# One instruction block for the whole program, and a new instruction order and PSUM plan in the third stage

## The reference, cut to what matters

```python
x = x + self_attention(_layernorm(x))                 # 16 heads of 8
x = x + cross_attention(_layernorm(x), ctx, mask)     # 16 heads of 64
x = x + ffn(_layernorm(x))                            # ffn below

def ffn(x):
    for i in range(6):
        x = attn_layer(shift_tokens(x), Wqkv[i], q_scale[i], k_scale[i], Wo[i]) + x
        x = ffn_layer(shift_tokens(x), ln_g[i], ln_b[i], W1[i], b1[i], W2[i], b2[i]) + x
    return x

def attn_layer(x, Wqkv, qs, ksc, Wo):      # 16 heads of 64, causal window of 32
    q, k, v = split(x @ Wqkv)
    q, k = l2norm(q) * qs, l2norm(k) * ksc
    q = q * cos * scale + rotate_half(q) * sin * scale
    k = k * cos / scale + rotate_half(k) * sin / scale
    return local_attention(q, k, v) @ Wo   # softmax(8 q k + mask) v

def ffn_layer(x, g, bln, W1, b1, W2, b2):
    a, gate = split(layernorm(x) * g + bln) @ W1 + b1
    return a * gelu(gate) @ W2 + b2
```

## Time and profile before

| what | value |
|---|---|
| median of 3 runs | 3522.41 us |
| profiled execution, device time | 3525.89 us |
| its span, first to last instruction | 3524.1 us |
| PE busy / weight loads | 96% / 71% |
| DVE, ACT, POOL busy | 80%, 79%, 70% |
| mean granted TensorE clock | 0.993 |

### The profile page before, as it was taken

The page is one execution under the profiler, slowest core; times in us unless marked ns, Lnnn a source line. Parts: engine busy times, 40 slices in busy tenths (PEclk is TensorE's granted clock), DMA queues, the critical chain, the costliest instruction groups (busy, mean ns, idle before and its releaser), DMA issues.

```text
span 3524.1 us, 120975 instructions
## 1 busy us (share of the span) xinstructions
PE 3377.9 (96%) x49605; PEld 2495.3 (71%) x49605; DVE 2811.5 (80%) x5297; ACT 2792.7 (79%) x5522; POOL 2475.5 (70%) x4812
## 2 busy tenths in 40 slices
PE   8989997999999999999999999999999999999997
PEld 5778774677777777777777777777777777777776
DVE  6834445888888888888888888888888888888885
ACT  5756664688888888888888888888888888888885
POOL 5622224777777777777777777777777777777774
PEclk9999998999999999999999999999999999999999
DMA  3000002444444444444444444444444444444441
GB/s 101 3 10 8 9 6 50 92 82 82 82 81 89 95 82 82 80 88 97 82 82 82 83 90 93 82 82 80 90 96 83 82 82 88 78 85 83 88 85 39
DMA packets 200382, 260.17 MB, mean 74 GB/s; under 512 B 123161, under 2 KB 145438, under 8 KB 199838
## 3 DMA queue, kind: packets, MB, share of 16 engines
q0 software_dynamic: 55296, 201.35, 30.4%
q1 hardware_dynamic: 143820, 50.88, 5.8%
q10 hardware_dynamic: 722, 0.21, 0.0%
HBM read 23.95 MB, written 2.10 MB: 7 GB/s over the span
## 4 chain that ended last, share of the span: by engine, by line
PE 78%; issue 2%; DVE 1%; POOL 1%; DMA 1%; ACT 0%; SPq 0%; POOLq 0%; DVEq 0%
PE bank L1032 18%; PE bank L1008 16%; PE bank L1083 10%; PE bank L1160 10%; PE bank L1128 7%; PE bank L1144 6%; PE bank L1103 5%; PE bank L1024 3%; PE bank L1098 2%; DVE R L1319 1%; DMA R<-R 1%; POOL R L1432 0%; POOL P L1444 0%; DVE ss L1332 0%; POOL P L1438 0%
## 5 line engine op out<-in xcount | busy, mean ns | idle before, releaser
L1319 DVE TENSOR_TENSOR R<-bank,tables 128x1024 f32<-128x1024 f32 x768 | 903.6, 1218 | 167.5 <-ACT sq L1219 127.4
L1032 PE MATMUL bank<-WA,xcT 128*128 128x512 f32 x1536 | 757.6, 596 | 1.8 <-ACT xcT L1194 1.8
L1008 PEld LDWEIGHTS bank<-ident,R 128*128 128x128 f32 x3072 | 371.6, 141 | 307.0 <-issue 299.9
L1444 POOL TENSOR_TENSOR P<-P,inv_sum 128x512 f32<-128x512 f32 x384 | 458.2, 1193 | 13.1 <-DVE inv_sum L1373 12.1
L1332 DVE TENSOR_REDUCE ss<-sq 128x16 f32<-128x1024 f32 x384 | 460.3, 1199 | 0.0
L1219 ACT ACTIVATE sq<-bank 128x512 f32<-128x512 f32 x768 | 438.2, 595 | 23.9 <-PE bank L1032 23.5
L1432 POOL TENSOR_TENSOR R<-R,rn 128x512 f32<-128x512 f32 x384 | 392.3, 1042 | 88.1 <-DMA R<-R 73.4
L1008 PE MATMUL bank<-ident,R 128*128 128x128 f32 x3072 | 429.8, 273 | 3.3 <-POOL R L1432 2.4
L1438 POOL TENSOR_TENSOR P<-P,rn 128x512 f32<-128x512 f32 x384 | 402.5, 1048 | 2.1 <-DVE P L1361 2.1
L1160 PE MATMUL bank<-WO,OT 128*128 128x128 f32 x3072 | 386.4, 279 | 1.7 <-ACT OT L1194 1.7
L1083 PE MATMUL bank<-WV,xcT 128*64 128x512 f32 x1536 | 376.0, 606 | 3.2 <-DVE R L1319 2.9
(11 more groups left out here) (154 smaller groups left out, 7082.5 us busy)
## 6 DMA issues: line engine op xcount, KB each, us to landing
R<-R POOLq DMA_DIRECT2D x384, 512.0 KB, 5.3
WA<-in_wqkv SPq DMA_DIRECT2D x24, 256.0 KB, 2.8
ystat<-Y SPq DMA_DIRECT2D x192, 32.0 KB
ystat<-Y SPq DMA_DIRECT2D x384, 15.8 KB
ys<-Y SPq DMA_DIRECT2D x192, 32.0 KB
ys<-Y SPq DMA_DIRECT2D x384, 15.8 KB
WV<-in_wqkv SPq DMA_DIRECT2D x6, 512.0 KB, 5.9
WO<-in_wo SPq DMA_DIRECT2D x6, 512.0 KB, 4.3
```

The costliest lines, as they stand in the source:

```text
L1008: return nc.tensor.transpose(dst, src, m.ident[:, :])
L1032: mm(b[QK_BANK[n, half]][:, :], m.xsT[:, t % 2, :], cols[:, half, :, :], start=True, stop=True)\
L1319: tt(both, src.unsqueeze(1).to_broadcast([128, 2, 16, 32]), tab.unsqueeze(2).to_broadcast([128, 2, 16, 32]), ALU.mult).then_inc(s.rotated. ...
L1444: tt(part, part, wide(m.inv_sum[:, t % 2, 8 * a:8 * a + 8]), ALU.mult).then_inc(s.normal.sem, 1)
```

## The change

It does three things.

- The four parts no longer make blocks of their own. They append their engine functions to five lists (`m.sync`, `m.tensor`, `m.scalar`, `m.vector`, `m.gpsimd`), and one block at the end of `build` runs each engine through its list. So there is no meeting of all engines between the parts.
- In the third stage the order of steps on PE, ACT, DVE and POOL is changed. On PE the values stand between head outputs and scores, and both groups of four transposed probabilities follow the scores. On POOL the two DMAs have two scalings between them instead of one, and the inverse deviation comes behind them.
- The PSUM banks of the third stage are given out anew, and the waits and semaphore counts follow from that.

No arithmetic is added or removed. The diff, cut to its core, without the change of indentation:

```diff
+        with nc.Block() as block:
+            @block.tensor
+            def _(pe):
+                for stage in m.tensor:
+                    stage(pe)
...
-    with nc.Block() as block:
-        @block.tensor
+    @m.tensor.append
         def _(pe):
...
-    QK_BANK = {(QUERIES, 0): 3, (QUERIES, 1): 6, (KEYS, 0): 1, (KEYS, 1): 2}
-    TURNED_IN, TURNED_OUT = b[4], b[6]
-    KT_BANK, QT_BANK, V_BANK = (b[7], b[0]), (b[7], b[4]), (b[1], b[4])
-    S_BANK, PT_BANK, PV_BANK = (b[5], b[6]), (b[0], b[0]), (b[4], b[3])
-    OUT, FF_BANK, FF_OUT = b[0], (b[2], b[1], b[7]), b[5]
+    QK_BANK = {(QUERIES, 0): 6, (QUERIES, 1): 5, (KEYS, 0): 7, (KEYS, 1): 1}
+    TURNED_IN, TURNED_OUT = b[6], b[5]
+    KT_BANK, QT_BANK, V_BANK = (b[2], b[4]), (b[0], b[3]), (b[2], b[5])
+    S_BANK, PT_BANK, PV_BANK = (b[0], b[7]), (b[6], b[5]), (b[4], b[6])
+    OUT, FF_BANK, FF_OUT = b[4], (b[2], b[1], b[3]), b[3]
...
             def keys(t, half):
                 if exists(t):
-                    if half == 1 and t < 2:
-                        at_least(pe, s.rotated.sem, s.rotated.upto((KEYS, 1), t))
+                if half == 0:
+                    at_least(pe, s.less.sem, s.less.upto(1, t - 1))
...
             def ff_in(t):
-                    pe.wait_ge(s.rotated.sem, s.rotated.upto((KEYS, 1), min(t + 8, N)))
+                at_least(pe, s.y, t)
...
                 queries(i, 0)
-                queries_turned(i - 1, 1)
                 queries(i, 1)
                 queries_turned(i - 1, 0)
+            queries_turned(i - 1, 1)
                 keys(i, 0)
                 keys(i, 1)
                 keys_turned(i - 1, 1)
-                keys_turned(i - 1, 0)
                 ff_out(i - 8)
-                probs_turned(i - 3, 1)
+            keys_turned(i - 1, 0)
                 normal_turned(i - 6)
                 head_outputs(i - 4)
-                scores(i - 1)
-                values(i, 0)
                 values(i, 1)
+            values(i, 0)
+            scores(i - 1)
+            probs_turned(i - 3, 1)
                 probs_turned(i - 3, 0)
                 ff_in(i - 7)
```

The end of ACT's list changes from `... exponents(i-2,0), outputs_out(i-4,0), probs_out(i-3,1), exponents(i-2,1), normalised(i-5), outputs_out(i-4,1), values_out(i,0), probs_out(i-3,0), values_out(i,1)` to:

```diff
+            values_out(i, 1)
                 exponents(i - 2, 1)
                 outputs_out(i - 4, 1)
+            outputs_out(i - 4, 0)
                 values_out(i, 0)
+            probs_out(i - 3, 1)
                 probs_out(i - 3, 0)
+            exponents(i - 2, 0)
+            normalised(i - 5)
```

DVE and POOL:

```diff
                 seeded(i)
                 maximum(i - 1, 0)
-                maximum(i - 1, 1)
-                less_maximum(i - 1, 1)
                 row_sums(i - 2, 0)
                 less_maximum(i - 1, 0)
-                inverse_sums(i - 2, 0)
-                attention_added(i - 4)
-                gated(i - 7)
                 row_sums(i - 2, 1)
+            maximum(i - 1, 1)
+            attention_added(i - 4)
                 inverse_sums(i - 2, 1)
+            gated(i - 7)
+            less_maximum(i - 1, 1)
+            inverse_sums(i - 2, 0)
...
                 queries_added(i)
+            probs_scaled(i - 3, 1)
                 probs_scaled(i - 3, 0)
                 keys_added(i)
+            inverse_deviation(i - 5)
                 inverse_lengths(i)
-                keys_scaled(i, 0)
                 keys_scaled(i, 1)
-                scores_scaled(i - 1, 1)
-                probs_scaled(i - 2, 1)
                 scores_scaled(i - 1, 0)
-                inverse_deviation(i - 4)
+            keys_scaled(i, 0)
+            scores_scaled(i - 1, 1)
```

More of the change, by code:

```diff
@@ new lines, in _ @@
+    @m.sync.append
+    def _(sp):
+        sp.dma_start(m.X[:, 0:8, :], x_tiles[:, 0:8, :]).then_inc(m.x_in[0], 16)
+        sp.wait_ge(zeroed, 1)
+        for i in range(SD):
+            off = i * (i + 1) // 2
+            sp.dma_start(m.tril[i:128:SD, 0:i + 1], m.params[:, off:off + i + 1],
+                         allow_slow_non_contiguous=True).then_inc(tril_in, 16)
+    @m.gpsimd.append
+    def _(pool):
+        pool.memset(m.tril[:, :], 0.0).then_inc(zeroed, 1)
+        pool.memset(m.ones[:, :], 1.0)
+        pool.memset(m.minus_half[:, :], -0.5)
+        pool.memset(m.spare[:, :], 0.0)
+        pool.memset(m.H[:, :, :, :], 1.0)
+        pool.memset(m.self_V, 1.0)
+        pool.memset(m.ystat[:, :, :], 0.0)
+        pool.memset(m.ys[:, :, :], 0.0)
@@ new lines, in _ @@
+    @m.vector.append
+    def _(dve):
+        dve.wait_ge(early, 16 * len(first))
+        dve.wait_ge(tril_in, 16 * SD)
+        dve.tensor_tensor(m.trilbd[:, :].rearrange("p (h j) -> p h j", j=SD),
+                          m.tril[:, :].unsqueeze(1).to_broadcast([128, HEADS, SD]),
+                          m.heads8[:, :].unsqueeze(2).to_broadcast([128, HEADS, SD]), ALU.mult).then_inc(made, 1)
+        dve.tensor_reduce(m.head_in4[:, :], m.heads8[:, :].rearrange("p (g j) -> p j g", j=4), AX.X, ALU.add)
+        dve.wait_ge(turned, 2)
+        dve.tensor_tensor(m.bias_row[:, :], m.borow[:, :], m.bank[2][0:1, 0:128], ALU.add)
@@ new lines, in _ @@
+    @m.tensor.append
+    def _(pe):
+        pe.wait_ge(made, 1)
+        pe.transpose(m.bank[0][:, 0:128], m.trilbd[:, :], m.ident[:, :]).then_inc(turned, 1)
+        pe.matmul(m.bank[2][0:1, 0:128], m.bvcol[:, :], m.woT_sb[:, :], start=True, stop=True).then_inc(turned, 1)
+        pe.wait_ge(copied, 1)
+        pe.matmul(m.bank[1][:, 0:128], m.trilT[:, :], m.trilT[:, :], start=True, stop=True).then_inc(turned, 1)
+    @m.scalar.append
+    def _(act):
+        for dst, src in first:
+            act.dma_start(dst, src, allow_slow_non_contiguous=True).then_inc(early, 16)
+        act.wait_ge(turned, 1)
+        act.activation(m.trilT[:, :], m.bank[0][:, 0:128], ACT.Copy).then_inc(copied, 1)
+        act.wait_ge(turned, 3)
+        act.activation(m.wqk[:, :], m.bank[1][:, 0:128], ACT.Copy)
```

1910 lines of the change are left out of this document (938 added, 972 removed).

## The result

The changed kernel takes 3392.3 us (median; 3390.8 to 3393.4), the kernel before on the same chip 3522.8. The ratio is 0.963, with a 95% interval of 0.961 to 0.965: 130 us less. The forecast was 70 us less, 3452, in a range of 3428 to 3508. So the sign was right and the size was not: the time lies 36 us under the low end.

A forecast was written before the change was run, and what follows sets the result against it. PE was taken to set the pace, losing time to instruction-fetch stalls before the scores. From the profiled 3525.9 us, 62.6 (third-stage rounds) and 7.8 (joins) gave 3455.5; the profiled execution being 3.5 above the median, 3452, range 3428 to 3508.

The forecast's parts named there:

- the stall: PE before the third stage's scores: a late instruction block, one stall in about three rounds; removing it gains 0.39 us per round.
- the third rival: Idle time before the scores is no instruction fetch and stays; only the barriers gain: 3514 us, chance 0.09.
- PE's sum stays 14.66: the same instructions at the same durations: Third stage: a PE round without a stall takes 14.66 us before and after the change.
- The 0.04 that the prediction left unexplained: Third stage, per round: part of the 0.43 us between 15.09 and 14.66 that the stalls' 0.39 did not cover.
- the 0.05 for a held block: Third stage's head outputs: charge per round, in us, for an instruction block held behind a 512 KB transfer; estimated 0.03.
- Joins: Setup and stage boundaries without barriers: waits of 2.63, 4.17 and 1.02 us go, 7.8 us in all, bounds 5 and 12.
- Transfers issued apart: POOL's two 512 KB transfers, third stage: each may hold instruction blocks up to 3 us, 6 in a row; charged 0.05 per round.
- The first rival: Third stage's head outputs: held blocks replace the stall, 0.25 to 0.3 us per round; 3490 us, chance 0.18 with small waits.
- The slower rival: Third stage: the chain from the late exponent through DVE to the keys sets the round; up to 3562 us, chance 0.13.

The follow-up runs named there:

- experiment 3: The kernel before, with the first half of the third stage's values moved between head outputs and scores on PE, all else unchanged: 3582.4 us, 1.017.
- experiment 5: The changed kernel with the third stage's head outputs computed twice over, into the same places: 3751.2 us, 1.064.
- Experiment 1: The kernel before, with the third stage's transposed ystat put in the bank of the second head outputs (b[3]) and its waits adapted: 3486.2 us, 0.989.
- (7): The changed kernel, but POOL issues the queries' transfer behind both scalings, directly ahead of the keys' transfer: 3407.7 us, 0.967.
- experiment 2: The changed kernel with one more PE wait, for ACT's last exponents of the round before, ahead of the ystat transpose: 3442.0 us, 0.976.
- experiment 6: The changed kernel with 96 already met semaphore waits added on PE between head outputs and values: 4722.5 us, 1.340.

## Why the prediction was right or wrong

**Right: the stall and what takes it away.** The stall before the scores is a late block of instructions. Taken away by work put between (experiment 3), brought back by dense work elsewhere (5), each time with one packet ahead of it; PE goes on 2.5 us after the packet's start in all these kernels (2.2 to 2.9 for nine in ten; 2.3 at the second place of experiment 5). The prediction had 2.2 and up to 2.8 with the delay. As it said would show it, the scores of the third stage have no idle time. The Trainium skill (Runtime: NRT & Kernel Launch, Instruction fetch mechanics) calls the crossing of a block "mostly hidden", since the engine goes through instructions slower than they arrive: the changed kernel agrees, where the densest 190 instructions take 3.4 us (the prediction had 3.5), and the kernel before and experiment 5, with 1.7 and 1.4 (the prediction had 1.8 for the first), do not. So the third rival fell.

**Wrong: "PE's sum stays 14.66: the same instructions at the same durations".** This is the step that failed. The 14.66 held 0.19 us of a wait for ACT and of the restart behind it, and 0.02 in the head outputs; the changed kernel's sum is 14.445. It took a wait of fixed length for the work's own time, since no row listed it. The new dealing of banks, which I had read as a mere consequence, took it away, perhaps with the new order of ACT's copies. Experiment 1 takes the same three steps down by 0.188 with a bank alone. Nearly a third of the gain came this way without being forecast; the right sign is no merit there. At 0.214 in some 190 rounds it is 41 of the 64 us by which the third stage was missed (126.6 against 62.6).

**Mis-sized: the stalls.** 0.39 less 0.05 per round were forecast, 0.437 measured: 0.097 more, 18 us. The 0.04 that the prediction left unexplained was of the same kind (stalls at `ystat`, head outputs and values, each 0.01 to 0.02 a round), and the 0.05 for a held block did not come. Its estimate before the allowance for the uncertain place was 0.03, still too high. The effect is real (5), but in the changed kernel no block is asked for at the wrong moment. The rest of the 64 us are the rounds: the gain holds in 190 and not in 184 (2 us), and 3 us in the emptying and in rounding.

**Joins.** 7.8 forecast; the pauses went by 8.3 to 8.8, the start of the third stage came 7.1 earlier, four blocks put back cost 7 to 10 by the times. ACT no longer waits for PE at the joins. The waits for POOL's `nmr` just ahead of them stayed, 2.97 and 6.04 us before, 3.37 and 6.20 now.

**"Transfers issued apart".** Charged at 0.05 per round for the block that might be held. The runs show it on another path: together they cost 15 us (7), by late keys. The prediction had not asked when the keys' transfer ends. The first rival, whose 0.25 to 0.3 a round needed requests under the transfer, did not come here; its mechanism is that of the second place in experiment 5.

**The slower rival** asked for DVE 0.5 us later than laid out. PE does not wait at the keys in the steady rounds (their step is 1.719 at the median, 1.82 at the most); the chain held. Where one step is moved without new banks (3), PE does wait for DVE in every round, at another place: the bank of the first keys.

The range was too narrow because each end was built from the known terms alone. The low end was all of the 0.43 above the undisturbed round and the largest join; that the undisturbed round itself could shrink had no place in it.

## What to carry to other kernels

Do not take the step between two runs of instructions for the time of the work: compare it with the least step of the same form elsewhere, and if it is 0.1 us longer in every round, look for another engine's copy that ends 0.1 us before it, in the same bank. An exchange of banks may then be worth more than an order. And look where the densest 190 instructions of an engine stand, and what large transfer runs when their block is asked for.

## What the hardware showed unexpectedly

- A wait that is already met cost PE 0.052 us where its sequencer was not ahead (96 of them, 5.02 us; no other number was tried), and nothing where it was (the additional wait ahead of the projection in experiment 1).
- A wait that ended late cost its length and 0.09 us more from the transpose to the second matmul behind it, 0.136 and 0.173 for 0.109 and 0.112 us in the kernel before, and the same 0.09 in experiment 2.
- From the start of an instruction packet to the instruction of PE that waited for it, it is 2.5 us. A 512 KB transfer by POOL held the packet back till its end, 28 times in experiment 5.
- In experiment 6 PE went through 96 waits from 2002.9 to 2007.8 us without a matmul; the granted clock was still 0.98 from 2003 to 2007. In the values and scores behind them it was 0.50 and 0.51 (2007.8 to 2011.4, 2012.5 to 2013.7), the level of 1.2 GHz, with PE busy, and then 1.00 (2014 to 2019).
- The first stage, with the same code, had a granted clock of 0.92 to 1.00 from one execution to the next, and its end moved by 10 us with it (second stage from 183.0 us at 1.00, from 193.5 at 0.93, in kernels with four blocks).
